# Another order of the same steps: three low-part subtractions, the lag tables and the beta additions change places in a fused AdaLN and FFN kernel

## The reference, cut to what matters

```
ctx    = causal_ema(x, tau_ctx)
wg     = sigmoid([x, ctx] @ Wg.T + bg);   gated = x * wg
h1     = gelu(x @ Wn1.T + bn1);           mod = 0.5 + sigmoid(h1 @ Wn2.T + bn2)     # 128 channels
traces[d] = causal_ema(gated * mod[..., d], tau_raws[d])
temporal  = sum over d of traces[d] * softmax(blend, axis=0)[d]
gate   = sigmoid(temporal @ Wtemp.T + btemp);  soma = gelu(x @ Wsoma.T + bsoma)
out    = layernorm((soma * gate) @ Wout.T) * gamma + beta
scores = out @ w_router; the better half of each batch's tokens goes through
         gelu(sel @ W1 + b1) @ W2 + b2, times sigmoid(score), added onto out at its place
return x + that
```

## Time and profile before

| | before |
|---|---|
| median of 3 runs (lowest to highest) | 177.53 us (177.35 to 177.87) |
| the profiled execution | 177.58 us, of which the span of its instructions is 175.9 us |
| TensorE busy | 164.4 us, 93% of the span |
| VectorE busy | 132.8 us, 76% |
| GpSimd busy | 128.2 us, 73% |
| ScalarE busy | 93.2 us, 53% |

### The profile page before, as it was taken

How to read it: one execution, slowest core, us unless ns; L and a number is a source line. 1 busy time by engine, 2 the same in 40 slices (tenths; PEclk the granted TensorE clock), 3 DMA queues, 4 the chain that set the end, 5 groups by cost and what they waited for, 6 DMA issues and landing times.

```text
span 175.9 us, 3161 instructions
## 1 busy us (share of the span) xinstructions
PE 164.4 (93%) x1076; PEld 123.8 (70%) x1076; DVE 132.8 (76%) x188; ACT 93.2 (53%) x160; POOL 128.2 (73%) x129
## 2 busy tenths in 40 slices
PE   6579899999999999999889999999999999899991
PEld 6343558597557775798564779787939869888881
DVE  1577698977985987987999798788866757868413
ACT  0682997676524724553353943535274479557420
POOL 7726804999335899689999998999889749199900
PEclk9978999999999999999999999999999999999999
DMA  3995000000000000000000000000000040040214
GB/s 98 248 254 152 0 4 0 0 2 6 0 0 0 4 0 0 0 4 0 0 0 0 4 0 2 0 4 0 0 6 0 0 121 0 4 119 0 83 40 119
DMA packets 12767, 5.60 MB, mean 32 GB/s; under 512 B 2864, under 2 KB 12624, under 8 KB 12752
## 3 DMA queue, kind: packets, MB, share of 16 engines
q1 hardware_dynamic: 11696, 5.20, 11.3%
q10 hardware_dynamic: 1056, 0.20, 0.7%
HBM read 3.30 MB, written 2.10 MB: 31 GB/s over the span
## 4 chain that ended last, share of the span: by engine, by line
PE 74%; DVE 10%; issue 5%; POOL 4%; ACT 2%; ACTq 2%; DVEq 0%; POOLq 0%
PE ring L1085 21%; PE ring L1158 6%; PE ring L1140 5%; PE ring L1041 5%; POOL ctx_acc L506 4%; PE ring L1057 4%; PE ring L1101 4%; PE ring L1042 4%; PE ring L1068 3%; PE ring L1020 3%; PE ring L1109 3%; PE ring L1168 3%; PE ring L1095 2%; PE ring L1145 2%; DVE mod_lo L814 2%
## 5 line engine op out<-in xcount | busy, mean ns | idle before, releaser
L506 POOL TENSOR_TENSOR ctx_acc<-ctx_acc,prod 128x640 f32<-128x640 f32 (+10 forms) x44 | 69.1, 1579 | 16.0 <-DVE prod L847 12.4
L847 DVE TENSOR_TENSOR prod<-ring,gm 128x640 f32<-128x640 f32 (+10 forms) x44 | 34.8, 818 | 7.2 <-PE ring L1085 6.1
L1085 PE MATMUL ring<-mod_hi,decayed_lo 128*128 128x512 f32 (+7 forms) x80 | 25.0, 377 | 0.9 <-DVE state L834 0.8
L1085 PE MATMUL ring<-mod_hi,decayed_hi 128*128 128x512 f32 (+7 forms) x80 | 22.5, 347 | 0.0
L1085 PE MATMUL ring<-mod_lo,decayed_hi 128*128 128x512 f32 (+7 forms) x80 | 22.5, 346 | 0.0
L834 DVE TENSOR_TENSOR state<-ring,blend_w 128x1024 f32<-128x1024 f32 x16 | 18.8, 1216 | 1.8 <-PE ring L1057 1.8
L1085 PEld LDWEIGHTS ring<-mod_hi,decayed_lo 128*128 128x128 f32 x80 | 13.9, 188 | 7.4 <-issue 5.1
L1085 PEld LDWEIGHTS ring<-mod_lo,decayed_hi 128*128 128x128 f32 x80 | 14.5, 188 | 1.2 <-issue 0.2
L1158 PE MATMUL ring<-w_sb,gm 128*128 128x128 f32 x128 | 15.2, 276 | 0.0
L1085 PEld LDWEIGHTS ring<-mod_hi,decayed_hi 128*128 128x128 f32 x80 | 14.5, 188 | 1.0
L1158 PEld LDWEIGHTS ring<-w_sb,gm 128*128 128x128 f32 x128 | 14.8, 192 | 0.3 <-ACT gm L710 0.2
(11 more groups left out here) (168 smaller groups left out, 357.4 us busy)
## 6 DMA issues: line engine op xcount, KB each, us to landing
x_nat<-in_x_dram SPq DMA_DIRECT2D x4, 512.0 KB, 5.4
out_dram<-x_nat SPq DMA_DIRECT2D x3, 512.0 KB, 3.2
w_sb<-in_L_ffn_W_dram SPq DMA_DIRECT2D x2, 256.0 KB, 4.2
out_dram<-x_nat SPq DMA_DIRECT2D x2, 256.0 KB, 2.4
down<-in_cond_dram SPq DMA_DIRECT2D x2, 64.0 KB, 4.7
prod<-in_L_cond_Wg_dram ACTq DMA_DIRECT2D x1, 128.0 KB, 4.4
prod<-in_L_cond_Wsoma_dram ACTq DMA_DIRECT2D x1, 64.0 KB, 4.5
bn<-in_L_cond_bn_dram ACTq DMA_DIRECT2D x4, 0.1 KB, 4.3
```

The source lines that it names most:

```text
L506: nc.gpsimd.tensor_tensor(dst, dst, packed(prod[:, n % NP, 0:width(r)], r, k), ALU.add).then_inc(acc_done, 1)
L847: nc.vector.tensor_tensor(dst, packed(slot(step), r, k), lagged(gated(r), r, k), ALU.mult).then_inc(read(step), 1)
L1085: last = nc.tensor.matmul(to[:, c], w[:, k, :], src[:, c], start=(i == 0), stop=(i == len(parts) - 1))
```

## The change

Only the list ORDER is another one; no step is added or taken out, and no line of code outside the list changes. Nearly all steps after the first ten change places somewhere. The first lines of the list before and after:

```
-decay:0 powers:0 decays:0 xt:0 turn_b:0 context:0 turn_a:0 xt:1 plus_beta:0 h1:0 soft:0 turn_c:0 context:1
-turn_f:0 wg:0 mod:0 gated:0 h1:1 table:0.0 table:0.1 table:0.2 low:0 split:0 ffn_w:0 table:0.3 mod:1 wg:1
-gated:1 early:0 unit:0.0 unit:0.6 unit:0.4 unit:0.7 split:1 xt:2 soma:0 h1:2 context:2 unit:0.8 low:1 unit:0.1
...
+decay:0 decays:0 xt:0 powers:0 turn_b:0 context:0 turn_a:0 soft:0 xt:1 h1:0 context:1 turn_c:0 wg:0 gated:0 h1:1
+mod:0 table:0.0 table:0.1 split:0 low:0 ffn_w:0 mod:1 table:0.2 rw:0 wg:1 gated:1 unit:0.0 unit:0.1 unit:0.3
+early:0 nat:0.0 split:1 unit:0.2 early:1 unit:0.6 plus_beta:0 nat:0.1 xt:2 unit:0.7 soma:1 soma:0 low:1
+context:2 state:0.0 unit:0.4 unit:1.0 xt:3 context:3 table:0.3 state:0.1 wg:2 wg:3 gated:2 duo:1.12 gated:3
...
+carry:0.0 unit:0.10 unit:1.8 turn_e:0 state:1.0 split:2 carry:1.1 sum:0 unit:1.1 back:0.0 unit:1.3 low:2
+unit:1.7 nat:2.0 nat:2.1 gate:0 soma_gate:0 unit:2.0 unit:2.1 unit:2.11 unit:2.3 out:0.0 stats:0.0 unit:1.11
+split:3 out:0.1 soma:2 early:3 back:1.1 low:3 state:2.1 carry:1.0 var:0 stats:0.1 unit:3.0 duo:3.12 sum:1
```

More of the change, by code:

```diff
@@ L60 @@
 ORDER = """
-decay:0 powers:0 decays:0 xt:0 turn_b:0 context:0 turn_a:0 xt:1 plus_beta:0 h1:0 soft:0 turn_c:0 context:1
-turn_f:0 wg:0 mod:0 gated:0 h1:1 table:0.0 table:0.1 table:0.2 low:0 split:0 ffn_w:0 table:0.3 mod:1 wg:1
-gated:1 early:0 unit:0.0 unit:0.6 unit:0.4 unit:0.7 split:1 xt:2 soma:0 h1:2 context:2 unit:0.8 low:1 unit:0.1
-mod:2 unit:0.2 nat:0.1 unit:0.5 nat:0.0 unit:1.0 early:1 unit:0.9 duo:1.14 xt:3 context:3 state:0.1 wg:2
-duo:1.13 duo:1.12 nat:1.1 carry:0.1 gated:2 state:0.0 duo:1.15 rw:0 unit:0.11 wg:3 unit:0.10 gated:3 nat:1.0
@@ L66 @@
[L66 to L75, removed]
@@ L76 @@
-residual:1 soma_gate:3 normed:2 turn_pick:1 score:2 out:3.0 bc:2 tie:2 pick:2 var:3 stats:3.0 residual:2 down:1
-out:3.1 stats:3.1 gather:2 scatter:1 up:2.0 up:2.1 score:3 normed:3 plus_beta:3 bc:3 tie:3 pick:3 turn_pick:2
-down:2 gather:3 scatter:2 up:3.0 up:3.1 turn_pick:3 down:3.0 down:3.1 scatter:3.0 residual:3 scatter:3.1
+decay:0 decays:0 xt:0 powers:0 turn_b:0 context:0 turn_a:0 soft:0 xt:1 h1:0 context:1 turn_c:0 wg:0 gated:0 h1:1
+mod:0 table:0.0 table:0.1 split:0 low:0 ffn_w:0 mod:1 table:0.2 rw:0 wg:1 gated:1 unit:0.0 unit:0.1 unit:0.3
@@ new lines @@
+early:0 nat:0.0 split:1 unit:0.2 early:1 unit:0.6 plus_beta:0 nat:0.1 xt:2 unit:0.7 soma:1 soma:0 low:1
+context:2 state:0.0 unit:0.4 unit:1.0 xt:3 context:3 table:0.3 state:0.1 wg:2 wg:3 gated:2 duo:1.12 gated:3
+unit:0.11 unit:1.5 duo:1.15 h1:2 h1:3 carry:0.1 mod:2 unit:1.10 unit:1.6 nat:1.1 duo:1.14 nat:1.0 turn_f:0
+unit:1.9 back:0.1 unit:1.4 unit:0.5 duo:1.13 early:2 turn_d:0 state:1.1 unit:0.9 unit:0.8 unit:1.2 mod:3
+carry:0.0 unit:0.10 unit:1.8 turn_e:0 state:1.0 split:2 carry:1.1 sum:0 unit:1.1 back:0.0 unit:1.3 low:2
@@ new lines @@
+unit:1.7 nat:2.0 nat:2.1 gate:0 soma_gate:0 unit:2.0 unit:2.1 unit:2.11 unit:2.3 out:0.0 stats:0.0 unit:1.11
+split:3 out:0.1 soma:2 early:3 back:1.1 low:3 state:2.1 carry:1.0 var:0 stats:0.1 unit:3.0 duo:3.12 sum:1
+unit:2.9 back:1.0 nat:3.1 score:0 unit:3.3 duo:3.15 state:2.0 bc:0 gate:1 duo:3.13 soma_gate:1 unit:2.2 unit:3.4
+unit:3.1 normed:0 tie:0 unit:3.10 pick:0 out:1.1 stats:1.1 soma:3 unit:2.4 out:1.0 duo:3.14 gather:0 carry:2.1
+carry:2.0 unit:2.6 unit:3.7 nat:3.0 unit:2.5 unit:3.5 var:1 unit:2.7 stats:1.0 back:2.0 state:3.1 unit:3.9
@@ new lines @@
+up:0.0 back:2.1 state:3.0 normed:1 unit:2.10 unit:2.8 turn_pick:0 carry:3.1 sum:2 residual:0 carry:3.0 unit:3.6
+unit:3.2 up:0.1 gate:2 score:1 bc:1 tie:1 soma_gate:2 unit:3.8 pick:1 down:0 unit:3.11 out:2.0 back:3.1 back:3.0
+out:2.1 stats:2.0 gather:1 sum:3 stats:2.1 scatter:0 var:2 turn_pick:1 soma_gate:3 gate:3 plus_beta:1 residual:1
+plus_beta:2 up:1.0 up:1.1 score:2 normed:2 out:3.0 var:3 bc:2 tie:2 pick:2 plus_beta:3 stats:3.0 down:1 out:3.1
+stats:3.1 gather:2 scatter:1 up:2.0 up:2.1 residual:2 residual:3 score:3 bc:3 tie:3 normed:3 pick:3 turn_pick:2
@@ L79 @@
+down:2 gather:3 scatter:2 up:3.0 up:3.1 turn_pick:3 down:3.0 down:3.1 scatter:3.0 scatter:3.1
 """
```

## The result

| | before | changed |
|---|---|---|
| median | 177.70 us (177.35 to 178.00, 4 executions) | 179.94 us (178.94 to 180.51, 4 executions) |
| the profiled execution | 177.58 us, span 175.9 | 180.51 us, span 178.7 |
| TensorE / VectorE / GpSimd / ScalarE busy | 164.4 / 132.8 / 128.2 / 93.2 us | 166.5 / 131.1 / 128.6 / 92.8 us |
| mean granted clock of TensorE, profiled execution | 0.988 | 0.981 |

The ratio is 1.0125 (95% interval 1.0098 to 1.0151): slower, on the side that was forecast and inside the range, but at 179.94 where 178.7 was forecast.

What follows compares the result with a forecast made beforehand. TensorE was taken to bound the kernel, with some 2.5 us of waits and head to win. The terms -0.35 + 0.43 + 1.4 + 1.4 + 0.2 - 1.7 - 0.2 gave +1.2, so 178.7 us beside the median; range 176.2 to 180.1.

Steps and rivals of the forecast that it cites:

- head, start of the lags: Head: turn_f leaves and mod:1 starts earlier, so the lags start some 0.35 us earlier; bounds 0.1 and 1.0.
- low:1, wait before `state`: Round 1's low part waits out GpSimd's lag 2 addition, so TensorE stands before state:0.0: +1.4 us, bounds 0.3 and 2.2.
- low:2, wait before the first lag of round 2: Third low part meets GpSimd's lag 1 addition, delaying the lag 7 product and unit:2.0: +1.4 us, bounds 0 and 2.2.
- low:3: Fourth low part, behind another product, with more TensorE steps before the lags needing it: +0.2 us, bounds 0 and 1.1.
- waits between 70 and 90 us that go: TensorE's old waits at the former places of low:2 and low:3, with 0.08 between 70 and 80, disappear: -1.7 us.
- tail: turn_pick:1 moves in front of gate:3, bringing down:1 forward on VectorE; half of its 0.46 us wait goes: -0.2 us.
- its first two matmuls (1.87 us) fall in the slow stretch either way: Head, wg:0 on TensorE: of its 0.43 us earlier start, 0.25 us is counted at its end.
- ScalarE reaches their high parts no sooner ...: nothing: Head: tables come some 2 us earlier on GpSimd, but ScalarE must do mod:0 first, so nothing is won.
- my widest bound: Head term: lags at most 1.0 us earlier, if TensorE's own work were all that counts there.
- (2): Subtractions find GpSimd idle, old collisions gone without new ones, decided at low:1: 176.1 us, chance 0.20.
- (1): low:2 slips in front of its addition and its 1.4 us go away: 177.3 us, chance 0.26.
- (3): GpSimd's additions run late as a whole, holding product buffers and gate:0: 180.2 to 180.7 us, chance 0.12.

Runs made afterwards that it cites:

- g1: Changed kernel with seven 128-column matmuls filling TensorE's head idle times, and split:1 and low:1 moved in front of the first product: 176.40 us, ratio 0.9942.
- e1: Changed kernel with the two gelu steps in front of low:1 in the other order, soma:0 before soma:1: 178.29 us, ratio 1.0037.
- e3: Changed kernel with four unused matmuls of 512 columns in TensorE's wait before state:0.0: 179.30 us, ratio 1.0111.
- e4: Changed kernel with the edits of e1 and e2 together: 177.55 us, ratio 0.9989.
- f1: Changed kernel with two unused matmuls of 512 columns in TensorE's wait before state:0.0: 178.43 us, ratio 1.0085.
- f3: Changed kernel with the fills of f1 and f2 together: 177.36 us, ratio 1.0008.
- e2: Changed kernel with low:2 one place later, behind the product of lag 7 of round 1: 179.29 us, ratio 1.0004.
- f2: Changed kernel with seven unused matmuls of 128 columns in TensorE's two idle times of the head: 178.79 us, ratio 1.0042.
- f4: Changed kernel with the two order edits of e4 and the head fill of f2: 176.36 us, ratio 0.9949.
- h1: Changed kernel with g1's order and head fill plus e2's move of low:2 behind the product of lag 7: 175.80 us, ratio 0.9898.
- g3: Kernel before the change with eight unused 128-column matmuls in its head idle times (four before xt:1, two before h1:0, two before ffn_w): 177.46 us, ratio 0.9999.
- g2: Kernel before the change with one move alone, plus_beta:0 from the head to behind unit:0.8: 177.56 us, ratio 0.9994.

## Why the prediction came out as it did

| step of the sum | forecast | measured in the profiled execution |
|---|---|---|
| head, start of the lags | -0.35 | -0.15 (24.39 for 24.54), the sum of several larger ones, below |
| turn_f among the lags | +0.43 | taken over, not measured apart |
| low:1, wait before `state` | +1.4 | +1.89 |
| low:2, wait before the first lag of round 2 | +1.4 | +1.26 |
| low:3 | +0.2 | 0 (1.23 us; it came first, and the addition waited) |
| waits between 70 and 90 us that go | -1.7 | -1.7 (the 1.26 idle left there is the new wait) |
| tail | -0.2 | 0 (the two waits before line 1168, 0.46 and 0.23 before, are 0.32 and 0.39) |
| half clock behind the wait before `state` | not in the sum | +1.5 |

These add to 3.2, against 2.9 between the two profiled executions.

The mechanism of the two stalls was right in each step that the rows show. Counted from the first lag matmul, the low part was to start at 9.8 and started at 10.5 (34.86 - 24.39), inside the same addition; `state` was to start at 13.6 and started at 14.4. The third low part was to start 2.3 us after `back:0.0` and did so 2.1 after (its end at 75.91), and the product behind it was to end at 6.0 and did at 5.7 (81.65). The Trainium skill (SBUF — State Buffer, section "Who interferes with whom") tells such a meeting as an exclusive lock on a port pair that the two engines share. The rows agree: in all profiles each low part of 1.3 us or more ended 1.07 to 1.09 us behind the end of the GpSimd instruction that it began in, and g1 shows the same subtraction short where no addition runs.

The step that failed is the account of the clock, and it failed twice. First, the sum had no term for what a new wait of TensorE does to the granted clock after it. The wait was priced as its own 1.4 us; in the profiled execution a half clock followed, and cost 1.5 more. e1, e3, e4, f1, f3 and g1, which fill that idle time or have less of it, have no execution with two stretches, and f3 shows the same two lags 1.5 us shorter; the changed kernel has two stretches in three of four executions, and e2, which keeps the wait, in four of seven. f2 and e2 also show that it need not come: in both profiles the wait stood (1.88 and 1.84 us) and the clock behind it stayed at 1.00. So the idle time makes the fall possible in some executions, and the median of a few is a draw among them; 178.7 was the time of one stretch (178.94), not of two.

Second, the head: "its first two matmuls (1.87 us) fall in the slow stretch either way" took the slow stretch of the profile before for a fixed part of the program, and "ScalarE reaches their high parts no sooner ...: nothing" followed from it. It is no fixed part.

To compare profiles one has to part them by one thing more, which the clock column doesn't show (it has 1.00 there): the first eight transposes of the program take 1.97 us in some profiles (changed, e1, e4, f4, h1) and 1.09 in the others. Here e1 and e3:

```profile
5.58 1.97 PE L1014 MATMUL ring<-ident,x_nat 128*128 128x128 f32 x8 [0.64 <-DMA x_nat<-in_x_dram]
```

```profile
5.58 1.09 PE L1018 MATMUL ring<-ident,x_nat 128*128 128x128 f32 x8 [0.64 <-DMA x_nat<-in_x_dram]
```

With the quick start the lags of the new order start at 22.17 without a half clock in the head (f2, f3, g1) and at 23.75 to 23.84 with one (f1, e2, e3); with the slow start at 22.73 to 23.01 without (e1, f4, h1) and at 24.39 to 24.50 with one (changed, e4). So the half clock costs the new order some 1.7 us there, and the slow start some 0.6. The old order starts its lags at 24.5 or 24.7 in either case in the two profiles compared here (both with the quick start): in g3 its tables, behind plus_beta:0, hold it. So the new order can gain some 2.4 us in the head (24.54 to 22.17), 1.4 more than my widest bound, and ties it to the clock: a half clock costs the kernel before 0.15 us (177.58 against 177.43) and this one some 1.7.

That the forecast's -0.35 lies near the -0.15 of the profiled execution is luck: there a gain of 2.4 was nearly used up by the half clock and the slow start. With that gain and the collisions' loss the new order is no slower than the old one at a full clock (ratios of 1.0008 in f3 and 0.9999 in g3), and it lost 1.25% because none of its four executions had a full clock. No run takes both limits, plus_beta:0 and the half clock, away from the old order at once; g2's two executions at 0.986, 1.3 us above its others, hint that without the first it would feel the second.

Of the rivals, the subtractions did not find GpSimd idle (2), low:2 did not slip in front of its addition (1), and the additions were not late as a whole (3): h1 and g1 won what the stalls cost. No rival had the clock in it; that was the gap in the list.

Open: executions of one kernel at one mean clock still spread by some 0.7 us. The slow start, 0.6 us, may be a part of that; it is there in five of the eleven profiles of the new order and in none of the three of the old one, and what causes it is not shown. Single executions of f2, f3 and g1 took some 2 us more at a mean clock of 1.00, and none of these was profiled. What decides, in one execution, whether the clock falls behind the same wait is not shown by these rows either.

## What to carry to other kernels

In this kernel a wait of TensorE cost more than its length when the clock fell behind it, so the price of a new wait has a second term, the matmuls behind it at half speed; it showed as executions of one kernel that fall into groups. Read the column of the granted clock in the profile before as one draw, not as part of the program, and ask of each stretch at half clock whether TensorE bounds there. Two instructions of VectorE and GpSimd that exclude each other are cheapest where GpSimd has nothing to do yet, and the next best is to put behind the blocked one what nobody waits for.

## What was not expected of the hardware

Seven matmuls of 128 columns whose results nobody reads, 2.0 us of TensorE in time that it mostly stood idle (1.06 and 0.94 us in f2's profile), kept the clock up in the head: with them, f3, f4, g1 and h1, in which the wait before `state` is filled or gone as well, have no execution under a mean clock of 0.994, in 39; e1 and e4, without the wait but also without the fill, have 15 of 24 at 0.990 or less, and f2, with the fill but also with the wait, 4 of 11. And a stretch at half clock, at another place in the head, cost 0.15 us in one order of the steps (177.58 against 177.43) and some 1.7 in the other.
